# Attention by units of a head pair and 512 queries: the maxima are split on GpSimd, their rows copied by ScalarE, and the SyncE and GpSimd queues reordered

## The chip, the cores and the metric

The kernel is one program on one core of a Trainium2 chip. The metric is the device time of one execution in microseconds; lower is better. A core has five engines with a queue each: TensorE (PE, matmul), VectorE (DVE), ScalarE (ACT), GpSimd (POOL) and SyncE (SP, which here only issues DMAs). They meet through semaphores.

## The reference, cut to what matters

Four stages with a layer norm behind each: a linear recurrence, a mixture of eight experts, multi-head attention, and a gated feed-forward block with quantised operands. The batch is 4 sequences of 1024 tokens of width 256. Only the attention changes:

```python
zn = (z - mu) / jnp.sqrt(var + 1e-05) * ln_w + ln_b
qkv = (zn @ W_qkv + b_qkv).reshape(b, n, 3, H, DH)      # here b = 4, n = 1024, H = 16 heads, DH = 16
scores = jnp.einsum('bhqd,bhkd->bhqk', q, k) * scale     # scale = 1/4
attn = jax.nn.softmax(scores, axis=-1)
msa = jnp.einsum('bhqk,bhkd->bhqd', attn, v)
out = msa_cat @ W_proj + b_proj
```

## The kernel before, in words

The first two stages run once for all tokens (the first 450 us). Then each of the four sequences b runs attention and the feed-forward block, one after the other.

Heads go by pairs p = 0 to 7; head a of a pair uses its own half of TensorE's rows (partitions 64a and up). Queries and keys are kept as a high and a low part, stacked into 48 rows per head (tiles Qs and Ks, four buffers for the pairs). SyncE fills a buffer with 12 DMAs (`stack(p)`, L432; for pair 0 three of them are GpSimd's).

A softmax needs the maximum of each query's scores. The scores are computed twice. First with queries on the partitions, 128 queries by 512 keys at a time (`score_max`, L976): 32 such matmuls a pair, 256 a sequence, called maxima here. VectorE reduces each to one column of MX (L1546). When all 32 of a pair are reduced, VectorE takes the negated maximum (L1550), splits it into a rounded high and a low part (L1551, L1552), TensorE transposes the small tile NMs (`turn_max`, L983), VectorE copies the transposed rows to MR (L1559), and SyncE's two DMAs (`maxima_row`, L440) put them as rows 49 and 50 under the queries. Then the second computation has keys on the partitions and the maximum already subtracted (`transposed_scores`, L1006: 128 keys by 512 queries, one matmul for each head), ScalarE applies the exponential to both heads at once (L708), and TensorE weighs the values (`weigh`, L1019, 4 calls in the program and 8 matmuls in the trace). A pair has 8 key tiles and 2 query halves, so 16 steps of transposed scores, exponential, weigh; a sequence has 128 steps. This text numbers them n = 0 to 127. ScalarE copies a pair's sums out of bank 7 (`evac_o`, L681), and the next pair's first `weigh` waits for that.

The maxima run ahead of the steps. TensorE issues 38 of the 256 ahead of the first step: 32 of pair 0 between the eight `values` matmul groups (L960) and 6 of pair 1, with filling matmuls between them (`keep_warm`, L1028, whose results nobody reads; `fill`, L1033). Behind that it puts 5 maxima beside every two steps up to step 12, then 4, so two a step, until none is left; from step 24 on (FIRST = 12 key tiles) they alternate with the steps one by one ("apart"), before that by two steps together. Once the first steps have begun the maxima rotate through three PSUM banks (4, 5, 6). The transposition takes a place ("slot") in this rotation, and whoever issues slot i waits until the content of slot i - 3 has been read (`slot_free`). Before, VectorE reads all slots, so one counter `sld` serves.

GpSimd, when pair 7's stack has landed, fetches the next sequence's input (L482) and copies two small tiles (L484, L485), and at steps of its own choosing (counter `pv`) issues four groups of four gathers (L492), which VectorE needs behind the last maximum. SyncE's order is stack 0, 1, 2, row 0, stack 3, then row p - 3 and stack p in turn.

The lines on which the prediction leans, from the kernel before:

```python
    before = [k for k in range(max(0, i - 8), i) if slot_bank(k) == slot_bank(i)]   # slot_free
    return before[-1] + 1 if before else 0
...
    F["nms"].wait(pe, b, p + 1)                  # turn_max, TensorE
    F["sld"].wait(pe, b, slot_free(i))
```

## Time and profile before

| | us |
|---|---|
| median of 3 runs | 1757.94 (1756.63 to 1764.83) |
| the profiled execution, its own time | 1757.24 |
| its span, first to last instruction | 1755.2 |
| PE busy | 1589.3 (91%) |
| DVE busy | 1345.5 (77%) |
| ACT busy | 873.3 (50%) |
| POOL busy | 258.8 (15%) |

Busy time is a sum over instructions of an engine; matmuls are pipelined and overlap, so a busy TensorE is not one at its peak. The last column of some rows names what ended an engine's idle time. The granted TensorE clock is 0.962 of full speed as a mean over the span.

### The profile page before, as it was taken

The numbers are of one execution on the slowest core, as the hardware profiler recorded it, in microseconds if no ns is written. First come the engines' busy times: TensorE is split into PE (matmuls) and PEld (weight loads), VectorE is DVE, ScalarE is ACT, GpSimd is POOL, SyncE is SP. The second block draws the span as 40 slices with busy tenths as digits, with TensorE's granted clock in tenths as the row PEclk, the third lists the DMA queues.
The fourth block names the chain that finished last, engine by engine and source line by source line (L and its number), as shares of the span: only waits on it lengthen the run. The fifth ranks groups of instructions, "written<-read, shape, count | busy, mean of one in ns | idle before, by whom it ended". The sixth has DMA issues, their size and how long they took to land.

```text
span 1755.2 us, 28045 instructions
## 1 busy us (share of the span) xinstructions
PE 1589.3 (91%) x10730; PEld 965.1 (55%) x10730; DVE 1345.5 (77%) x2629; ACT 873.3 (50%) x1294; POOL 258.8 (15%) x255
## 2 busy tenths in 40 slices
PE   5987999995799998899999989999998999999795
PEld 1757899994353336565433557543336655333564
DVE  3575555542599986889998689899978989996696
ACT  1213444441347775153777723367782344778412
POOL 0144233223100120201003030100202010000020
PEclk8988999998799999999999989999998999999998
DMA  3126877784322310004222000322200032110000
GB/s 134 49 72 213 258 251 245 249 245 148 59 35 37 68 38 1 1 10 88 38 38 74 2 0 1 79 37 38 75 19 1 1 72 41 34 28 2 1 0 24
DMA packets 80175, 123.03 MB, mean 70 GB/s; under 512 B 13530, under 2 KB 55771, under 8 KB 80043
## 3 DMA queue, kind: packets, MB, share of 16 engines
q1 hardware_dynamic: 70666, 93.46, 20.4%
q0 software_dynamic: 9376, 27.80, 5.5%
q8 instruction: 85, 1.39, 0.3%
q14 instruction: 48, 0.39, 0.1%
HBM read 76.84 MB, written 18.61 MB: 54 GB/s over the span
## 4 chain that ended last, share of the span: by engine, by line
PE 76%; DVE 14%; ACT 4%; issue 3%; DMA 1%; POOL 1%; SPq 1%; DVEq 0%; ACTq 0%; POOLq 0%
PE PS L1019 14%; PE PS L976 13%; PE PS L901 7%; PE PS L1141 7%; PE PS L889 6%; PE PS L1006 6%; PE PS L1151 5%; DVE MX L1546 4%; PE PS L946 3%; PE PS L960 2%; ACT Pb L708 2%; PE PS L839 2%; PE PS L1028 2%; PE PS L1100 1%; PE PS L1177 1%
## 5 line engine op out<-in xcount | busy, mean ns | idle before, releaser
L1546 DVE TENSOR_REDUCE MX<-PS 128x1 f32<-128x512 f32 x1024 | 634.2, 682 | 37.1 <-PE PS L976 34.9
L708 ACT ACTIVATE Pb<-PS 128x1024 f32<-128x1024 f32 x512 | 509.0, 1025 | 171.2 <-PE PS L1006 167.7
L976 PE MATMUL PS<-Ks,Qs 48*128 48x512 f32 x1024 | 381.4, 456 | 13.6 <-DVE MX L1546 11.3
L1006 PE MATMUL PS<-Qs,Ks 50*128 50x512 f32 x1024 | 334.1, 455 | 14.2 <-ACT Pb L708 11.4
L1019 PE MATMUL PS<-Pb,V 128*32 128x256 f32 x4096 | 308.6, 390 | 1.2 <-ACT Pb L708 0.2
L976 PEld LDWEIGHTS PS<-Ks,Qs 48*128 48x128 f32 x1024 | 160.6, 184 | 220.0 <-DVE MX L1546 159.9
L1019 PEld LDWEIGHTS PS<-Pb,V 128*32 128x32 f32 x4096 | 90.4, 108 | 155.0 <-ACT Pb L708 75.4
L1006 PEld LDWEIGHTS PS<-Qs,Ks 50*128 50x128 f32 x1024 | 137.0, 185 | 50.2 <-ACT Pb L708 36.1
L901 PE MATMUL PS<-Pb,OT 128*128 128x256 f32 x624 | 141.0, 379 | 0.0
L889 PE MATMUL PS<-Ks,Qs 128*128 128x256 f32 x936 | 127.3, 294 | 6.3 <-DVE Ks L1426 6.3
L889 PEld LDWEIGHTS PS<-Ks,Qs 128*128 128x128 f32 x936 | 119.5, 197 | 8.6 <-DVE Ks L1426 7.5
L901 PEld LDWEIGHTS PS<-Pb,OT 128*128 128x128 f32 x624 | 115.8, 190 | 14.0
L1141 PE MATMUL PS<-wgT,XT 128*128 128x352 f32 x256 | 98.0, 535 | 15.3 <-DVE OT L1644 12.3
L473 POOL DMA_INDIRECT OT<-x_mid,idx x78 | 80.3, 1029 | 197.3 <-PE PS L878 158.9
L621 ACT ACTIVATE Qs<-Pb 128x1024 fp32r<-128x1024 f32 x39 | 41.3, 1060 | 120.4 <-DMA Pb<-W 120.4
L1151 PE MATMUL PS<-wdT,Pb 128*128 128x256 f32 (+1 forms) x384 | 96.1, 393 | 2.0 <-ACT Pb L761 2.0
L1151 PEld LDWEIGHTS PS<-wdT,Pb 128*128 128x128 f32 (+1 forms) x384 | 71.0, 192 | 26.6 <-issue 11.3
L632 ACT ACTIVATE OT<-PS,b1t 128x256 f32<-128x256 f32 x156 | 64.8, 470 | 38.6 <-PE PS L889 38.6
L1141 PE MATMUL PS<-wuT,XT 128*128 128x352 f32 x256 | 81.8, 463 | 0.0
L1141 PEld LDWEIGHTS PS<-wgT,XT 128*128 128x128 f32 x256 | 54.1, 222 | 44.3 <-DVE OT L1644 13.3
L738 ACT ACTIVATE OT<-PS 128x704 f32<-128x704 f32 x32 | 24.2, 756 | 104.5 <-PE PS L1141 104.5
L1422 DVE TENSOR_TENSOR Qs<-Pb,Qs 128x1024 fp32r<-128x1024 f32 x39 | 47.7, 1224 | 28.5 <-ACT Qs L621 28.0
(288 smaller groups left out, 1912.9 us busy)
## 6 DMA issues: line engine op xcount, KB each, us to landing
Pb<-W SPq DMA_DIRECT2D x78, 512.0 KB
y_slot<-V SPq DMA_DIRECT2D x39, 256.0 KB
Qs<-Qh SPq DMA_DIRECT2D x128, 64.0 KB, 2.3
Ks<-Kh SPq DMA_DIRECT2D x120, 64.0 KB, 2.3
V<-b SPq DMA_DIRECT2D x39, 128.0 KB
XT<-x_mid POOLq DMA_DIRECT2D x4, 1024.0 KB
out<-Pb POOLq DMA_DIRECT2D x4, 1024.0 KB, 6.7
OT<-xT SPq DMA_DIRECT2D x2, 1024.0 KB, 6.2
```

The costliest lines, as they stand in the source:

```text
L473: C[("xa", "xb", "xc")[k % 3]].inc(pool.indirect_dma_start(Xm[k % 3][:, a, :], None, x_mid[:, :], bass.IndirectOffsetOnAxis(idx[:, SA * k ...
L632: C["hr"].inc(act.activation(HTm[k % 2][:, hc, :], PS[:, 2 + 2 * (k % 2) + hc // 2, hc % 2 * ST:(hc % 2 + 1) * ST], ACT.Relu, bias=b1t[:, ...
L708: F["ex"].inc(act.activation(Pb[:, kt % 2, 2 * qh:2 * qh + 2, :], PS[:, 2 * qh:2 * qh + 2, :], ACT.Exp, scale=0.25))
L889: ins = pe.matmul(PS[:, 2 + 2 * (k % 2) + hc // 2, hc % 2 * ST:(hc % 2 + 1) * ST], w[k % 2][:, c, hc * P:(hc + 1) * P], x[k % 2][:, c, :], ...
L901: ins = pe.matmul(PS[:, 6 + k % 2, a * D:(a + 1) * D], HTm[k % 2][:, hc, a * P:(a + 1) * P], W2t[k % 2][:, hc, :], start=(hc == 0), stop=( ...
L946: ins = pe.matmul(o, wqkv[:, kc, w * D + c * P:w * D + (c + 1) * P], tokens, start=(kc == 0), stop=(kc == DC - 1))
L976: F["slp"].inc(pe.matmul(PS[:, slot_bank(i), :], Qs[rows, p % NB, t * P:(t + 1) * P], Ks[rows, p % NB, kh * HALF:(kh + 1) * HALF], start=T ...
L1006: ins = pe.matmul(PS[:, 2 * qh + a, :], Ks[rows, p % NB, kt * P:(kt + 1) * P], Qs[rows, p % NB, qh * HALF:(qh + 1) * HALF], start=True, st ...
L1019: ins = pe.matmul(PS[32 * j:32 * j + 32, 7, qh * QW:(qh + 1) * QW], V[:, kt, 2 * p + a, :], Pb[:, kt % 2, 2 * qh + a, c * QW:(c + 1) * QW] ...
L1141: ins = pe.matmul(PS[:, 2 * w + a, 0:IH], XT[:, c, t * P:(t + 1) * P], wT[:, c, a * IH:(a + 1) * IH], start=(c == 0), stop=(c == DC - 1))
L1151: ins = pe.matmul(PS[:, 6 + t % 2, 0:D], HT[0:k, c, :], wdT[0:k, c, :], start=(c == 0), stop=(c == IC - 1))
L1546: F["sld"].inc(dve.tensor_reduce(MX[:, p % 2, a, t, kh:kh + 1], PS[:, slot_bank(i), :], AX.X, ALU.max))
```

## The change

A unit is now a pair and 512 queries: 16 units u a sequence, of 16 maxima each (UN = 16). What was done once a pair is done once a unit:

- VectorE takes the negated maxima of the unit's four query tiles (one instruction, now issued one maximum late: behind maximum 16(u + 1), which is the next unit's first).
- GpSimd makes the high and the low part (`split_maxima`).
- TensorE transposes 16 rows instead of 32. The slot of unit u lies ahead of maximum 16(u + 1) + 6 (LATER = 6), for unit 0 ahead of maximum 17.
- ScalarE copies the rows to MR (`maxima_rows`), behind the exponential of the step in whose course the transposition is issued (`turn_step`), and raises a new counter `mrc`. The user of the slot three further on waits for `mrc` instead of `sld`.
- SyncE sends two DMAs a unit, on counters `mrow0` and `mrow1` by query half; steps 8u to 8u + 7 belong to unit u, so all 8 key tiles of one query half are now done before the other half.

The first step now comes behind 24 maxima (UN + START = 16 + 8). The values are no longer interleaved with filling matmuls; of `keep_warm` 2 + 7 * 3 are left. All steps are "apart", weigh of step n - 2 stands behind the transposed scores of step n, and at a pair's change weigh is left out of one step and done twice in the next. SyncE's order is stack 0, 1, row 0, stack 2, row 1, stack 3, row 2, then row, stack, row for each further pair. GpSimd's fetch and gathers now stand behind the splits of units 11 to 14.

```diff
-LEAD, START = 12, 6
-APART, PVS = 4, 2
-SOON, LATER = 1, 4
+LEAD, START = 14, 8
+GATHER = 11
+SOON, LATER = 1, 6
...
-        UN = 2 * TT * 2
-        SLOTS = NP * UN + NP
+        UN = 2 * TT
+        NU = 2 * NP
+        QT = TT // 2
+        SLOTS = NU * UN + NU
...
+        slot_use = {unit_slot(n): ("sld", n + 1) for n in range(NU * UN)}
+        slot_use.update({turn_slot(u): ("mrc", u + 1) for u in range(NU)})
...
-            return before[-1] + 1 if before else 0
+            return slot_use[before[-1]] if before else None
+
+        LAST = (NU * UN - UN - LEAD) // 2
+
+        def ahead_of(n):
+
+            return UN + min(LEAD + 2 * n, START + 5 * n // 2)
+
+        def turn_step(u):
+
+            if u + 1 == NU:
+                return LAST + 1
+            return next(n for n in range(NU * KT) if ahead_of(n + 1) > UN * (u + 1) + LATER)
...
-                for p in range(NB - 1):
+                stack(0)
+                stack(1)
+                maxima_row(0)
+                for p in range(2, NB):
                     stack(p)
-                maxima_row(0)
-                stack(NB - 1)
+                    maxima_row(p - 1)
                 for p in range(NB, NP):
-                    maxima_row(p - NB + 1)
+                    maxima_row(2 * (p - NB) + NB - 1)
                     stack(p)
-                for p in range(NP - NB + 1, NP):
-                    maxima_row(p)
+                    maxima_row(2 * (p - NB) + NB)
+                for u in range(2 * (NP - NB) + NB - 1, NU):
+                    maxima_row(u)
...
+                def split_maxima(u):
+
+                    F["neg"].wait(pool, b, u + 1)
+                    if u:
+                        F["slp"].wait(pool, b, turn_slot(u - 1) + 1)
+                    F["nmh"].inc(pool.tensor_copy(NMs[:, :, 0, :], NM[:, u % 2, :, :]))
+                    F["nmh"].wait(pool, b, u + 1)
+                    F["nms"].inc(pool.tensor_tensor(NMs[:, :, 1, :], NM[:, u % 2, :, :], NMs[:, :, 0, :].bitcast(F32), ALU.subtract))
+
+                for u in range(NU):
+                    split_maxima(u)
+                    if more and u == GATHER:
+                        F["vv"].wait(pool, b, TT)
+                        F[f"stk{NB - 1}"].wait(pool, b, NP // NB * STK)
+                        fetch(b + 1)
+                        F["cp"].wait(pool, b, 1, 1)
+                    if more and GATHER <= u < GATHER + TT // 2:
+                        gathers((u - GATHER,))
...
+                def maxima_rows(u):
+                    i = turn_slot(u)
+                    F["slp"].wait(act, b, i + 1)
+                    if u >= 2:
+                        F[f"mrow{u % 2}"].wait(act, b, 16 * 2 * (u // 2))
+                    F["mrc"].inc(act.activation(MR[:, u % 2, :], PS[0:2 * TT, slot_bank(i), 0:P], ACT.Copy))
+
+                maxima_rows(0)
+                for n in range(NU * KT):
+                    F["bp"].wait(act, b, n + 1)
+                    if n >= 4:
+                        F["pv"].wait(act, b, n - 3)
+                    F["ex"].inc(act.activation(weights_of(n), PS[:, 2 * (n % 2):2 * (n % 2) + 2, :], ACT.Exp, scale=0.25))
+                    if n > 2 and n % (2 * KT) == 1:
+                        evac_o(n // (2 * KT) - 1)
+                    for u in range(1, NU):
+                        if turn_step(u) == n:
+                            maxima_rows(u)
...
-                for t in range(1, TT):
-                    maxima(4 * t + 1)
-                    F["vv"].wait(pe, b, t)
-                    keep_warm(2, 1)
-                    maxima(4 * t + 3)
+                for t in range(1, 5):
+                    maxima(3 * t + 3)
                     values(t)
                 maxima(UN)
+                for t in (5, 6):
+                    values(t)
+                maxima(UN + SOON)
+                values(7)
                 F["vv"].wait(pe, b, TT)
-                keep_warm(18)
-                maxima(UN + SOON)
-                keep_warm(7, 1)
+                keep_warm(2, 1)
...
+                for n in range(NU * KT):
+                    if n == LAST + 2:
+                        turn_max(NU - 1)
+                    maxima(ahead_of(n) + 1)
+                    if n < 2:
+                        fill(2)
+                    transposed_scores(n)
+                    for k in range(ahead_of(n) + 2, ahead_of(n + 1) + 1):
+                        maxima(k)
+                        if n < 2:
+                            fill(2)
+                    if n < 2:
+                        continue
+                    if n == 2 or n % (2 * KT) != 2:
+                        if n > 3 and n % (2 * KT) == 3:
+                            weigh(n - 3)
+                        weigh(n - 2)
...
-                    link(dve.tensor_reduce(NM[:, :, :], MX[:, p % 2, :, :, :], AX.X, ALU.max, negate=True))
-                    link(dve.tensor_copy(NMs[:, :, 0, :], NM[:, :, :]))
-                    F["nms"].inc(dve.tensor_tensor(NMs[:, :, 1, :], NM[:, :, :], NMs[:, :, 0, :].bitcast(F32), ALU.subtract))
...
+                row_maxima(0, 1)
+                for u in range(NU):
+                    row_maxima(UN * u + 1, min(UN * (u + 1) + 1, NU * UN))
+                    negated_maxima(u)
```

## Rows read from the trace of the kernel before

**Rows 1.** The page's costliest group: busy us, mean ns, idle before

```profile
L1546 DVE TENSOR_REDUCE MX<-PS 128x1 f32<-128x512 f32 x1024 | 634.2, 682 | 37.1 <-PE PS L976 34.9
```

**Rows 2.** Second sequence by stretches: us, busy PE, PEld, DVE, ACT, POOL, clock, DMA

```profile
880.00:920.00 40.00, 39.90 (x364) 15.05 (x366) 38.67 (x69) 31.36 (x33) 0.00 (x0) 1.00 0.25 42
920.00:960.00 40.00, 38.56 (x339) 14.87 (x337) 35.99 (x65) 28.40 (x31) 13.74 (x17) 1.00 0.23 68
```

**Rows 3.** Timeline, one loop step (from 876.16), TensorE: start us, us, instruction

```profile
876.16 0.50 PE L976 MATMUL PS<-Ks,Qs 48*128 48x512 f32 x1
876.16 0.74 PE L1006 MATMUL PS<-Qs,Ks 50*128 50x512 f32 x2
...
876.83 0.64 PE L1019 MATMUL PS<-Pb,V 128*32 128x256 f32 x8
877.40 0.50 PE L976 MATMUL PS<-Ks,Qs 48*128 48x512 f32 x1
```

**Rows 4.** Timeline, the same step, ScalarE and VectorE

```profile
876.93 1.03 ACT L708 ACTIVATE Pb<-PS 128x1024 f32<-128x1024 f32 x1 [0.21 <-PE PS L1006]
...
875.46 6.25 DVE L1546 TENSOR_REDUCE MX<-PS 128x1 f32<-128x512 f32 x10
```

**Rows 5.** Timeline, start of attention, VectorE

```profile
796.54 19.22 DVE L1546 TENSOR_REDUCE MX<-PS 128x1 f32<-128x512 f32 x32
815.79 0.19 DVE L1550 TENSOR_REDUCE NM<-MX 128x16 f32<-128x32 f32 x1
...
817.14 0.28 DVE L1559 CAST MR<-PS 32x128 fp32r<-32x128 f32 x1
```

**Rows 6.** Timeline, the same stretch, TensorE

```profile
820.25 0.50 PE L1006 MATMUL PS<-Qs,Ks 50*128 50x512 f32 x2 [0.61 <-DMA Qs<-MR]
```

**Rows 7.** Timeline, the same stretch, SyncE's queue

```profile
808.11 0.59 SPq L432 DMA_DIRECT2D Ks<-OT  x1
817.45 1.36 SPq L440 DMA_DIRECT2D Qs<-MR  x2
```

**Rows 8.** Timeline, ScalarE, the last four exponentials of the sequence

```profile
989.45 3.78 ACT L708 ACTIVATE Pb<-PS 128x1024 f32<-128x1024 f32 x4 [0.19 <-PE PS L1006]
```

**Rows 9.** Groups by line and form, ScalarE and GpSimd: busy us, mean ns, idle

```profile
L761 ACT ACTIVATE Pb<-PS 64x128 f32<-64x128 f32 x32 | 8.6, 270 | 0.0
...
L485 POOL COPY svb<-sv 128x16 f32<-128x16 f32 x4 | 0.8, 204 | 0.0
```

**Rows 10.** Timeline, a transposition inside the loop, TensorE

```profile
903.54 0.50 PE L976 MATMUL PS<-Ks,Qs 48*128 48x512 f32 x1
...
905.17 0.28 PE L983 MATMUL PS<-ident,NMs 128*32 128x128 f32 x1
...
906.97 0.49 PE L976 MATMUL PS<-Ks,Qs 48*128 48x512 f32 x1
```

**Rows 11.** Timeline, TensorE, at steps 12, 24, 106 and behind the last

```profile
841.01 0.72 PE L1006 MATMUL PS<-Qs,Ks 50*128 50x512 f32 x2
...
857.20 0.40 PE L1006 MATMUL PS<-Qs,Ks 50*128 50x512 f32 x2
...
969.77 1.12 PE L1006 MATMUL PS<-Qs,Ks 50*128 50x512 f32 x4
...
991.87 2.05 PE L1019 MATMUL PS<-Pb,V 128*32 128x256 f32 x32
```

**Rows 12.** Timeline, TensorE, at a pair's change

```profile
891.93 0.49 PE L976 MATMUL PS<-Ks,Qs 48*128 48x512 f32 x1
...
894.86 0.50 PE L976 MATMUL PS<-Ks,Qs 48*128 48x512 f32 x1
```

**Rows 13.** Timeline, VectorE, last work before the heads' normalisation, and that

```profile
986.33 0.17 DVE L1483 TENSOR_SCALAR ve<-mv 128x8 f32<-128x8 f32 x1
995.77 0.26 DVE L1596 RECIPROCAL rc<-PS 128x16 f32<-128x16 f32 x1 [9.27 <-PE PS L1090]
```

**Rows 14.** The stack's line on SyncE's queue: min, median and max ns

```profile
L432 SPq DMA_DIRECT2D Qs<-Qh x128: 555/590/1837, 463.8 to 1554.2; - x128
```

More of the change, by code:

```diff
@@ L512, in sequence @@
             def sequence(b, more):
-                if more:
-                    F["vv"].wait(pool, b, TT)
-                    F[f"stk{NB - 1}"].wait(pool, b, NP // NB * STK)
-                    fetch(b + 1)
-                    F["cp"].wait(pool, b, 1, 1)
-                    for g in range(TT // 2):
-                        F["pv"].wait(pool, b, PVS * (APART * g + 5 * KT - 4))
-                        gathers((g,))
+                def split_maxima(u):
[14 more added lines that the diff above has]
+                        gathers((u - GATHER,))
                 w, nb = 2 * D, 2 * D // BLK
@@ L973, in score_max @@
                     if slot_free(i):
-                        F["sld"].wait(pe, b, slot_free(i))
+                        F[slot_free(i)[0]].wait(pe, b, slot_free(i)[1])
                     rows = slice(ROW * a, ROW * a + STACK)
@@ L988, in maxima @@
                 def maxima(upto):
-                    while issued[0] < min(upto, NP * UN):
+                    while issued[0] < min(upto, NU * UN):
                         n = issued[0]
@@ L997, in maxima, with transposed_scores @@
                         issued[0] += 1
-                def transposed_scores(p, kt, qh):
-                    n = 2 * (KT * p + kt) + qh
+                def transposed_scores(n):
+                    u, kt = n // KT, n % KT
+                    p, qh = u // 2, u % 2
+                    if kt == 0:
+                        F[f"mrow{qh}"].wait(pe, b, 16 * 2 * (p + 1))
                     if n >= 2:
@@ L1005, in transposed_scores, with weigh @@
                         rows = slice(ROW * a, ROW * a + MROWS)
-                        ins = pe.matmul(PS[:, 2 * qh + a, :], Ks[rows, p % NB, kt * P:(kt + 1) * P],
+                        ins = pe.matmul(PS[:, 2 * (n % 2) + a, :], Ks[rows, p % NB, kt * P:(kt + 1) * P],
                                         Qs[rows, p % NB, qh * HALF:(qh + 1) * HALF], start=True, stop=True)
                     F["bp"].inc(ins)
-                def weigh(m, qh):
-                    p, kt = m // KT, m % KT
-                    if kt == 0 and p:
+                def weigh(n):
+                    u, kt = n // KT, n % KT
+                    p, qh = u // 2, u % 2
+                    if kt == 0 and qh == 0 and p:
                         F["ov"].wait(pe, b, p)
-                    F["ex"].wait(pe, b, 2 * m + qh + 1)
+                    F["ex"].wait(pe, b, n + 1)
                     for c in range(2):
@@ L1053, in sequence @@
                 F["vm"].wait(pe, b, 1)
-                FIRST = 12
-                LAST = (NP * UN - UN - LEAD) // 4
-                for m in range(NP * KT):
-                    p, kt = m // KT, m % KT
-                    if kt == 0:
-                        F["mrow"].wait(pe, b, 16 * 2 * (p + 1))
-                    ahead = UN + min(LEAD + 4 * m, START + 5 * m)
-                    step = UN + min(LEAD + 4 * (m + 1), START + 5 * (m + 1)) - ahead
-                    apart = FIRST <= m < LAST
-                    for qh in range(2):
-                        if apart:
-                            maxima(ahead + 2 * qh + 1)
-                        transposed_scores(p, kt, qh)
-                        maxima(ahead + (2 if not qh else step if apart else 3))
-                        if m == 0:
-                            fill(2)
-                        if apart:
-                            weigh(m - 1, qh)
-                    if not apart:
-                        for qh in range(2 if m else 0):
-                            weigh(m - 1, qh)
-                        for n in range(ahead + 4, ahead + step + 1):
-                            maxima(n)
-                            if m == 0:
-                                fill(2)
-                        if m == LAST:
-                            turn_max(NP - 1)
-                for qh in range(2):
-                    weigh(NP * KT - 1, qh)
+                for n in range(NU * KT):
[8 more added lines that the diff above has]
+                        if n < 2:
+                            fill(2)
+                    if n < 2:
[4 more added lines that the diff above has]
+                        weigh(n - 2)
+                for n in range(NU * KT - 2, NU * KT):
+                    weigh(n)
                 F["ov"].wait(pe, b, NP)
```

85 lines of the change are left out of this document (33 added, 52 removed).

## The prediction

> **What bounds the kernel now.** I read the page first, then the chain of waits, then the busy time by stretches, and last the timeline of each engine in the second sequence (the four are alike; all times below are of it). The page's largest group is VectorE's reduction of the maxima [rows 1], but in the loop TensorE is busy for 39.90 of 40 us and VectorE for 38.67 [rows 2]: both are nearly full, TensorE a little more. The clock is granted in full in these stretches (1.00, the level of 2.4 GHz).
>
> One step of the loop shows why. It lasts 876.16 to 877.40, 1.24 us: a maximum and a transposed score start together, because they use different rows of the array, a second such couple follows, then weigh from 876.83 [rows 3]. VectorE takes 6.25 us for ten maxima, 0.62 each; unhindered it takes 19.22 / 32 = 0.60 [rows 4, 5]. ScalarE's exponential starts 0.77 us after the step's start and takes 1.03 [rows 3, 4], so it idles 0.21 a step.
>
> Ahead of the loop it is otherwise. VectorE begins at 796.54 and must do 32 maxima; the negation is at 815.79, the copy of the rows ends at 817.42, SyncE issues the row's DMAs at 817.45, and the first transposed score starts at 820.25, 2.83 us behind the copy [rows 5 to 7]. In these 24 us TensorE's filling matmuls do nothing useful. Behind the last maximum (step 106) the steps run by ScalarE: four exponentials in 3.96 us with the idle time ahead, 0.99 a step [rows 8].
>
> The sum is made against the profiled execution's own 1757.24 us (span 1755.2 and 2.0 around it), 0.7 under the median.
>
> **Part 1, the start and the catching up.** The first step needs 17 reductions instead of 33. 796.54 + 17 x 0.60 + 0.08 gives 806.8; the negation 0.19; GpSimd's two small instructions about 0.20 each, the nearest row being its copy of 128x16 [rows 9], with handovers 0.5 in all; TensorE's transposition 0.28 [rows 10]; ScalarE's copy about 0.27, by its copy of 64x128 out of PSUM [rows 9]. That is 808.3 with handovers. SyncE's queue holds only stacks 0 and 1 ahead of the row and has been past stack 2 at 808.7 even in the old order [rows 7], so it is free. With the same 2.83 us the first step could begin at 811.1; the 8 maxima ahead of it hold it to about 811.5. Before: 820.25, so 8.7 earlier.
>
> But 24 maxima have then been issued, not 38. Up to step 12 VectorE sets the pace: it starts again at about 808.4 with maximum 17, and 37 maxima bring it to 830.6; the second negation and the second transposition's slot add 0.5, and TensorE's lead takes as much off. Step 12 begins at 830.6 against 841.01 [rows 11]: **-10.4 us**.
>
> The negation runs off VectorE's path from here on: 0.2 a unit where it had 0.6 and a copy of 0.28 a pair.
>
> **Part 2, the transposition in the loop.** This is where I expect most of the gain to go. A transposition takes one of three slots. In the kernel before, VectorE frees it within its own order. The two steps from 903.54 to 906.97 with one of them inside take 3.43 instead of 2.48: 0.95 a pair [rows 10].
>
> Now ScalarE frees it, and its copy stands behind the exponential of the very step in which the transposition is issued. With the transposition's start as 0: the step's couples start at 0.21, its exponential at 0.21 + 0.77 = 0.98, the copy, overlapping the exponential's last 0.1 as the exponentials do (3.78 for four) [rows 8], runs 1.90 to 2.17. The third slot on is the first maximum of the next step, which TensorE would reach at 1.58 (1.24, the transposition's 0.21, and 0.13 by which VectorE's negation delays the second couple). It waits until 2.21 (a handover of 0.04, as between the copy at 817.42 and SyncE), and behind it in TensorE's queue wait the next transposed scores, and so the next exponential. Cost: 2.21 - 1.24 = 0.97 us a unit. The bounds: 0.34 if the wait isn't there, 1.3 if handovers are three times as long.
>
> A pair's change costs 2.93 - 2.48 = 0.45 now [rows 12]. Weigh left out of one step and doubled in the next lets ScalarE's copy of 0.6 pass; I take 0.2 (bounds 0 and 0.45).
>
> Steps 12 to 24: 12 x 1.24 + 2 x 0.97 + 0.2 = 17.0, before 857.20 - 841.01 = 16.2 [rows 11]: **+0.8**.
>
> Steps 24 to the last maximum: before 969.77 - 857.20 = 112.6 for 82 steps, which is 101.7 of steps, 5 x 0.95, 5 x 0.45 and 3.9 left over. The left-over lies where GpSimd issues gathers: TensorE's 39.90 of 40 us falls to 38.56 in that stretch [rows 2]; I keep it, since the gathers only move by nine steps. Now the last maximum is at step 113: 89 x 1.24 + 11 x 0.97 + 6 x 0.2 + 3.9 = 126.2. The tail before is 22 steps, from 969.77 to the end of the last weigh at 993.9 [rows 11], 24.1 = 22 x 0.99 + 2.3. Now 15 x 0.99 + 2.3 = 17.2. Together 143.4 against 136.7: **+6.7**.
>
> Sum: -10.4 + 0.8 + 6.7 = **-2.9 us a sequence, -11.6 in all: 1745.6**.
>
> **What I cost at nothing.** The next sequence's combination on VectorE ends at 986.33 and is wanted at 995.77 [rows 13]; it would start 4 us later (last maximum at 973.8 instead of 969.8), so end at 990.3, and be wanted 2.9 earlier, at 992.9: 2.6 us of cover are left; what is late beyond that counts in three of the four sequences. GpSimd: four gathers stand behind a unit's split, about 1 us each by its 13.74 us for 17 instructions [rows 2], and the next split is due 8 steps, 10 us, after. A unit's negation ends 1.45 into step 8u - 7 and the transposition stands at the start of step 8u - 4, 2.3 us on, of which the split takes 0.6: 1.7 to spare. Fetch now stands behind split 11, where pair 7's stack has landed. SyncE: a stack is 12 x 0.63 us by the row's median of 0.59 and a gap [rows 14], 9 with the row ahead of it; the next row is due 13 us after the last. The row in the loop: copy done 2.17 behind the transposition, 2.83 more for the DMA, 5.0; its reader is due at 2.21 + 3 x 1.24 = 5.93. Cover 0.9.
>
> GpSimd and VectorE might get into each other's way, which would undo the split's move. VectorE reads the maxima from PSUM while GpSimd works; in the stretch with gathers its mean for a maximum can't be told from that without [rows 2]. The Trainium skill (Perfetto Trace Analysis, "Optimizing Scalar/DVE Operations") warns that GpSimd and VectorE share an SBUF port, so that moving work between them might not help; SBUF — State Buffer, "Who interferes with whom", exempts a reduction on this chip. By the warning the move would gain VectorE nothing, by the exemption it costs nothing; the sum takes the second.
>
> **The rivals.** *A, the slot is free in time.* If the copy gets ahead of the exponential's end, or the slack absorbs it, a transposition costs 0.34: 13 x 0.63 and 0.3 at unit 1 are 8.5 a sequence, 34 in all: 1712. For it: ScalarE idles 0.21 a step. Against: that idle time lies ahead of the exponential, and the queue is in order. Chance 0.15.
>
> *B, slower: the rows come late.* Sixty times (15 a sequence) the steps wait for a row whose cover is 0.9 us. If a row takes 1.3 us longer inside the loop than at the start, 0.4 is lost each time, 24 us: 1770. It decides from 0.35 us a unit, where the sum reaches 1767. For it: single DMA issues took 1.84 instead of 0.59 [rows 14], and a row has two of them; fetch's 1 MB goes out close to row 11. Against: SyncE is otherwise idle then. Chance 0.12.
>
> *C, the two engines collide.* If VectorE stands still for GpSimd's 0.4 a unit, 16 x 4 x 0.4 = 26 us is the most; the wait behind the transposition, in which VectorE is idle for 0.63 anyway, should cover half: about 1758, no change. Chance 0.08.
>
> *D, the fillers are missed.* TensorE's clock stays at its higher level now while fillers run between the values. If it fell to the lower level for the first 12 steps, their matmuls would take twice as long, about 8 us a sequence: 1778. The gaps I see in the new order are under 0.5 us. Chance 0.03.
>
> **How the numbers follow.** My forecast has 0.62, with its own range 1735 to 1758 (0.1 us on each of 52 transpositions is 5 us; 1 us in a sequence's start is 4). Half a per cent, 8.8 us, is about what can be told from no change. Of the forecast 0.43 lies under 1749.2 and 0.19 within; with A faster is 0.58; with C and a part of B same is 0.28; slower 0.14, B and D. The range of 8 in 10 reaches to A below and to the edge of B above: 1709 to 1764. The predicted time is 1745.6.
>
> **What would show it.** Right: the first transposed score 15 us after VectorE's first maximum (23.7 now), give or take 1; behind each transposition the first maximum of the next step waiting 0.6 us for ScalarE; steps of 1.24; the last weigh 2.9 us earlier than now, counted from VectorE's first maximum. Wrong: no such wait (A); transposed scores waiting for the row's DMA at every eighth step (B); maxima of 0.7 us where GpSimd splits (C); steps longer than 1.24 without a wait.

## The result and the profile after

The changed kernel takes 1747.59 us in the median of its runs (1738.82 to 1770.11), the kernel before 1758.88 (1753.09 to 1764.83) beside it: a ratio of 0.9944, with a 95% interval of 0.9925 to 0.9963. Forecast were 1745.6 us, so -11.6 for a measured -11.3. The profiled execution took 1747.05 us, with a span of 1745.3: 9.9 less than before. A ratio here, and its interval, leave out the runs that lie over 1.5% above their kernel's fastest (here the one at 1770.11), and so can differ a little from the quotient of the medians.

The page's groups of VectorE's maxima, ScalarE's exponentials and TensorE's scores (busy us, mean ns, then the idle time ahead of them and who ended it) answer to [rows 1]; the last line is TensorE's own group in the page before:

```profile
L1581 DVE TENSOR_REDUCE MX<-PS 128x1 f32<-128x512 f32 x1024 | 636.5, 683 | 70.1 <-PE PS L1018 69.2
L748 ACT ACTIVATE Pb<-PS 128x1024 f32<-128x1024 f32 x512 | 518.9, 1026 | 180.0 <-PE PS L1051 179.4
L1018 PE MATMUL PS<-Ks,Qs 48*128 48x512 f32 x1024 | 389.8, 455 | 35.0 <-ACT MR L741 28.8
...
L976 PE MATMUL PS<-Ks,Qs 48*128 48x512 f32 x1024 | 381.4, 456 | 13.6 <-DVE MX L1546 11.3
```

A maximum costs what it did (683 ns against 682), but VectorE now idles 70.1 us ahead of them instead of 37.1. TensorE's maxima waited for VectorE before, 11.3 us in all. Now they wait for another engine: for 28.8 us TensorE stands still until ScalarE has copied a unit's rows.

The start of the second sequence, timeline of all engines (VectorE's first maximum is at 794.35; [rows 5 to 7] answer to it):

```profile
806.18 0.28 PE L1025 MATMUL PS<-ident,NMs 128*16 128x128 f32 x1
...
806.49 0.27 ACT L741 ACTIVATE MR<-PS 16x128 fp32r<-16x128 f32 x1 [0.80 <-PE PS L1025]
806.78 1.36 SPq L462 DMA_DIRECT2D Qs<-MR  x2
806.92 4.28 DVE L1581 TENSOR_REDUCE MX<-PS 128x1 f32<-128x512 f32 x7 [1.91 <-PE PS L1018]
...
810.15 0.50 PE L1051 MATMUL PS<-Qs,Ks 50*128 50x512 f32 x1
```

The first transposed score starts 15.80 us behind the first maximum, where it was 23.71: 7.9 earlier.

A step of the loop with a transposition in it, same view ([rows 10] answer to it):

```profile
873.11 0.28 PE L1025 MATMUL PS<-ident,NMs 128*16 128x128 f32 x1
...
874.09 1.02 ACT L748 ACTIVATE Pb<-PS 128x1024 f32<-128x1024 f32 x1 [0.42 <-PE PS L1051]
...
875.01 0.25 ACT L741 ACTIVATE MR<-PS 16x128 fp32r<-16x128 f32 x1
...
875.32 0.49 PE L1018 MATMUL PS<-Ks,Qs 48*128 48x512 f32 x1 [0.50 <-ACT MR L741]
```

From the transposition to the next step's first maximum it is 875.32 - 873.11 = 2.21 us. The copy stands behind the exponential in ScalarE's queue, and the maximum waits for the slot that the copy frees.

Counted from the first maximum to the start of ScalarE's last copy of the heads, the attention of the four sequences took 198.70, 197.45, 197.57 and 193.65 us before and takes 192.97, 193.46, 193.52 and 190.39: 17.0 less in sum. Some 1.2 of it is not the change's: in the kernel before the clock fell to 0.50 for 3.4 us (at 658.5) late in the first sequence. The span shows 9.9. The stretches between, which the change does not touch, came out 3.6 us longer ahead of the first sequence, 1.7 between them and 1.9 behind the last, in these two executions.

The last sequence is shorter in both kernels, and it alone issues no gathers for a next one. Timeline around the fourth gather of a unit, changed kernel, second sequence:

```profile
931.78 0.96 POOL L517 DMA_INDIRECT Kh<-y_slot,posb  x1 [0.30 <-issue]
...
933.56 2.48 DVE L1581 TENSOR_REDUCE MX<-PS 128x1 f32<-128x512 f32 x4 [1.29 <-PE PS L1018]
933.60 1.94 ACT L748 ACTIVATE Pb<-PS 128x1024 f32<-128x1024 f32 x2 [1.36 <-PE PS L1051]
934.30 0.50 PE L1018 MATMUL PS<-Ks,Qs 48*128 48x512 f32 x1 [0.65 <-DVE MX L1581]
```

VectorE and ScalarE, which read different banks, get nothing from TensorE for 1.29 and 1.36 us, and come back together 0.8 us after GpSimd's fourth gather has ended. The other three groups of gathers show the like: ScalarE comes back after 1.77, 1.09 and 1.75 us of idle time at 944.34, 955.75 and 967.63, each time 0.9 to 1.0 us behind a fourth gather's end, and VectorE beside it after 0.53, 1.50 and 0.51. I call this a stop below. Not all of this idle time is lost: at the three later places, behind a transposition, ScalarE is idle for 0.82 us in the fourth sequence too.

It is not bound to the fourth gather. In the third group ScalarE is late already before that one starts:

```profile
953.49 1.02 ACT L748 ACTIVATE Pb<-PS 128x1024 f32<-128x1024 f32 x1 [1.42 <-PE PS L1051]
953.83 0.96 POOL L517 DMA_INDIRECT Kh<-y_slot,posb  x1 [0.31 <-PE PS L1018]
```

This exponential comes 1.50 us behind the transposition (at 951.99). In the other two sequences with gathers the same one comes 1.54 and 1.53 behind it, in the fourth 0.97.

### The profile page after: what moved, and what is told of

Same layout as the page of the kernel before. It is cut to its first block, busy times and chain, and to the rows that moved or that the text cites. A ratio compares the mean times of both kernels' runs of the same rounds, so it can differ in the third digit from the quotient of the medians.

```text
span 1745.3 us, 28266 instructions
## 1 busy us (share of the span) xinstructions
PE 1568.2 (90%) x10646; PEld 940.9 (54%) x10646; DVE 1328.9 (76%) x2565; ACT 889.5 (51%) x1358; POOL 285.7 (16%) x383
## 4 chain that ended last, share of the span: by engine, by line
PE 71%; DVE 17%; issue 6%; ACT 3%; DMA 2%; POOL 1%; SPq 1%; ACTq 0%; DVEq 0%; POOLq 0%
PE PS L1065 13%; PE PS L1018 13%; PE PS L1176 7%; PE PS L943 7%; PE PS L931 6%; PE PS L1051 6%; DVE MX L1581 6%; PE PS L1186 5%; PE PS L988 3%; PE PS L1002 2%; PE PS L881 2%; PE PS L1135 1%; PE PS L1212 1%; DMA Pb<-W 1%; PE PS L920 1%
## 5 line engine op out<-in xcount | busy, mean ns | idle before, releaser
L1581 DVE TENSOR_REDUCE MX<-PS 128x1 f32<-128x512 f32 x1024 | 636.5, 683 | 70.1 <-PE PS L1018 69.2
L748 ACT ACTIVATE Pb<-PS 128x1024 f32<-128x1024 f32 x512 | 518.9, 1026 | 180.0 <-PE PS L1051 179.4
L1018 PE MATMUL PS<-Ks,Qs 48*128 48x512 f32 x1024 | 389.8, 455 | 35.0 <-ACT MR L741 28.8
L1051 PE MATMUL PS<-Qs,Ks 50*128 50x512 f32 x1024 | 360.4, 452 | 0.0
L1065 PE MATMUL PS<-Pb,V 128*32 128x256 f32 x4096 | 320.5, 390 | 0.5
L1065 PEld LDWEIGHTS PS<-Pb,V 128*32 128x32 f32 x4096 | 83.8, 108 | 162.0 <-ACT Pb L748 87.1
L1051 PEld LDWEIGHTS PS<-Qs,Ks 50*128 50x128 f32 x1024 | 143.5, 185 | 24.4 <-ACT Pb L748 19.8
L543 POOL CAST NMs<-NM 128x8 fp32r<-128x8 f32 x64 | 12.7, 199 | 597.7 <-DVE NM L1588 597.7
L1186 PEld LDWEIGHTS PS<-wdT,Pb 128*128 128x128 f32 (+1 forms) x384 | 71.0, 192 | 26.8 <-issue 11.3
```

The costliest lines, as they stand in the source:

```text
L748: F["ex"].inc(act.activation(weights_of(n), PS[:, 2 * (n % 2):2 * (n % 2) + 2, :], ACT.Exp, scale=0.25))
L1018: F["slp"].inc(pe.matmul(PS[:, slot_bank(i), :], Qs[rows, p % NB, t * P:(t + 1) * P], Ks[rows, p % NB, kh * HALF:(kh + 1) * HALF], start=T ...
L1051: ins = pe.matmul(PS[:, 2 * (n % 2) + a, :], Ks[rows, p % NB, kt * P:(kt + 1) * P], Qs[rows, p % NB, qh * HALF:(qh + 1) * HALF], start=Tru ...
L1065: ins = pe.matmul(PS[32 * j:32 * j + 32, 7, qh * QW:(qh + 1) * QW], V[:, kt, 2 * p + a, :], weights_of(n)[:, a, c * QW:(c + 1) * QW], star ...
L1186: ins = pe.matmul(PS[:, 6 + t % 2, 0:D], HT[0:k, c, :], wdT[0:k, c, :], start=(c == 0), stop=(c == IC - 1))
L1581: F["sld"].inc(dve.tensor_reduce(MX[:, p % 2, a, t, kh:kh + 1], PS[:, slot_bank(i), :], AX.X, ALU.max))
```

## The experiments

Twelve kernels ran, on three chips. The kernel before ran beside them at 1760.54 us in the first group of four, 1758.38 in the second and 1748.87 in the third; each ratio is to its own. A unit's time is the distance between two splits of the maxima, read in the profiled execution (so a split that GpSimd issues late shifts it); "units 11 to 14" are those with gathers behind them.

### First group: which part of the change costs what

**The changed kernel again.**

> The changed kernel itself, as the yardstick of this call. Ratio to the kernel before 0.994 (0.992 to 0.996), as in its own timing.

1749.24 us (1740.08 to 1753.63), ratio 0.9924 [0.9900, 0.9949]. A unit without gathers alternates between 11.13 and 10.87 us, 22.00 for two. In this execution something is new. Windows in the third sequence (us, busy PE, PEld, VectorE, ScalarE, GpSimd, granted clock, DMA share, GB/s):

```profile
1260.00:1270.00 10.00, 8.73 (x81) 3.43 (x76) 7.94 (x14) 7.23 (x9) 4.22 (x6) 0.97 0.18 53
1270.00:1280.00 10.00, 10.00 (x60) 3.30 (x52) 6.03 (x12) 4.34 (x5) 2.73 (x5) 0.50 0.05 15
```

Behind a group of gathers the granted clock falls to 0.50, the level of 1.2 GHz, for 30.7 us (1269.3 to 1300.0). That sequence took 204.7 us of attention instead of 193.5.

**The copy ahead of the exponential** (units 2 to 14; the lines `+` come before the wait for the step's scores):

```diff
 for n in range(NU * KT):
+    for u in range(2, NU - 1):
+        if turn_step(u) == n:
+            maxima_rows(u)
     F["bp"].wait(act, b, n + 1)
...
     F["ex"].inc(act.activation(weights_of(n), ...))
...
-    for u in range(1, NU):
+    for u in (1, NU - 1):
         if turn_step(u) == n:
             maxima_rows(u)
```

> The changed kernel with ScalarE's copy of the rows of units 2 to 14 ahead of the exponential of the same step instead of behind it. ScalarE is idle for 0.21 us there and the transposition is done 0.7 us before that exponential can start, so by my theory the wait of TensorE for the slot goes and a transposition costs about 0.34 us instead of 0.97: 13 x 0.63 = 8 us a sequence, 33 in all, so about 0.975 of the kernel before. The rival (the slot's wait only takes the place of time that VectorE needs for its maxima anyway) expects no change: 0.994. In between, if VectorE becomes the limit at 16 x 0.62 a unit.

1747.2 us (1731.4 to 1775.56), ratio 0.9893 [0.9865, 0.9922], where 0.975 was expected. Timeline, a step with a transposition:

```profile
874.28 0.28 PE L1028 MATMUL PS<-ident,NMs 128*16 128x128 f32 x1
...
874.73 0.25 ACT L741 ACTIVATE MR<-PS 16x128 fp32r<-16x128 f32 x1
...
875.26 1.02 ACT L751 ACTIVATE Pb<-PS 128x1024 f32<-128x1024 f32 x1 [0.28 <-PE PS L1054]
...
875.91 0.49 PE L1021 MATMUL PS<-Ks,Qs 48*128 48x512 f32 x1
```

From the transposition to the next maximum it is 1.63 us instead of 2.21, with no wait. Two units take 20.65 instead of 22.00, and the undisturbed fourth sequence 181.94 instead of 190.47: 8.5 us less, which is what the prediction's rival A asked for (8.5 a sequence). The time shows little of it, because the first three sequences gave it back (198.49, 196.03 and 206.39 us). Windows of the second:

```profile
920.00:930.00 10.00, 10.00 (x93) 3.95 (x93) 9.11 (x16) 7.96 (x10) 4.99 (x9) 1.00 0.37 119
930.00:940.00 10.00, 8.90 (x56) 2.77 (x48) 6.35 (x11) 4.77 (x5) 2.62 (x5) 0.63 0.15 47
940.00:950.00 10.00, 10.00 (x57) 3.39 (x53) 5.33 (x10) 4.60 (x6) 2.23 (x3) 0.50 0.17 50
950.00:960.00 10.00, 10.00 (x61) 3.75 (x59) 6.32 (x11) 5.60 (x6) 3.80 (x6) 0.51 0.10 30
```

and the timeline at its beginning:

```profile
931.44 1.89 DVE L1584 TENSOR_REDUCE MX<-PS 128x1 f32<-128x512 f32 x3 [1.47 <-PE PS L1021]
931.49 1.94 ACT L751 ACTIVATE Pb<-PS 128x1024 f32<-128x1024 f32 x2 [1.81 <-PE PS L1054]
932.19 0.18 PEld L1021 LDWEIGHTS PS<-Ks,Qs 48*128 48x128 f32 x1 [1.54 <-DVE MX L1584]
932.19 0.51 PE L1021 MATMUL PS<-Ks,Qs 48*128 48x512 f32 x1 [1.10 <-DVE MX L1584]
```

A stop, 1.10 us of idle TensorE behind it, and then the lower clock from 932.5 to 959.9, in which TensorE is busy for 10.00 of 10 us and does 57 to 61 matmuls where it had done 93.

**The rows' copy on VectorE, as before the change.** `maxima_rows` moves from ScalarE's loop to VectorE's, just ahead of the maximum whose slot follows the transposition.

> The changed kernel with the copy of the rows given back to VectorE, in its order just ahead of the maximum whose slot follows the transposition, as in the kernel before; the split stays on GpSimd. By my theory the place of the copy behind the exponential is what costs, so this gains too: VectorE does 16 x 0.60 + 0.2 + 0.25 = 10.05 us a unit, TensorE 9.92 + 0.34 = 10.26, a transposition costs 0.4 to 0.6: 5 to 7 us a sequence, 0.980 of the kernel before. If ScalarE's copy was right to relieve VectorE (rival), this is slower than the changed kernel: over 0.994.

1746.95 us, from only four runs: 1728.51 and 1732.74 at a mean clock of 0.946, 1761.15 and 1764.85 at 0.928 and 0.920. Too few and too far apart for a ratio; 0.980 was expected, and the two quicker runs are at 0.983. The fourth sequence took 181.76 us, the others 189.24, 195.91 and 195.97 with the same falls of the clock behind gathers. Who copies does not matter, then; that the copy is not behind an exponential does.

**The split on VectorE, as before the change.**

```diff
-F["nmh"].inc(pool.tensor_copy(NMs[:, :, 0, :], ...))
-F["nms"].inc(pool.tensor_tensor(NMs[:, :, 1, :], ...))
+F["nmh"].inc(dve.tensor_copy(NMs[:, :, 0, :], ...))
+F["nms"].inc(dve.tensor_tensor(NMs[:, :, 1, :], ...))
```

> The changed kernel with the split of the maxima given back to VectorE, the copy of the rows stays on ScalarE. It puts 0.4 us a unit on VectorE. By my theory VectorE is idle behind each transposition for 0.6 us anyway, so that inside the loop it costs little, 0 to 0.15 us a unit, and the first transposition comes a little earlier: within 0.992 to 1.000 of the kernel before. If the move of the split is what the change lives on (rival), each unit costs 0.4 more: 25 us, 1.008.

1773.42 us (1771.82 to 1777.55), ratio 1.0083 [1.0065, 1.0101]: slower than the kernel before. Two units take 22.66 us, 0.33 more each; the two instructions are 0.17 each. I had counted them as covered by VectorE's idle 0.6 us behind a transposition, and expected 0.992 to 1.000; none of them is covered. The split stands two steps ahead of the transposition (at 872.82, the transposition at 875.45), and the idle time comes only behind it; that the maxima held up there are what costs is my reading, no run isolated it. That is some 4 us a sequence (197.3 against 193.5). The rest of the 24 us to the changed kernel goes with the clock: all four runs have a mean granted clock of 0.950 to 0.952, where runs of the changed kernel reach 0.963 to 0.965, and in the profiled one it fell for 34 us behind unit 1's transposition in the fourth sequence, far from any gather. Ahead of that fall TensorE had waited only 0.18 and 0.24 us for VectorE.

### Second group: the gathers

Three kernels with the copy ahead, and one of another question.

**One row a gather, plain.** In the attention each of the 16 gathers becomes `pool.dma_start(dst[0:1, t, :], y_slot[r:r + 1, :])`.

> The row copy stands ahead of the same step's exponential, as in the copy-ahead kernel (where a unit without gathers took 10.33 us instead of 11.00), and each of the 16 gathers of the next sequence's rows that GpSimd issues within the attention brings one row by a plain transfer instead of 128 by index (the next sequence computes on rows that are not its own; the work is the same). Theory (the gathers stop both readers of PSUM for 1 to 2 us, and TensorE's granted clock falls to its lower level behind such a stop): units 11 to 14 take 10.33 us too, no stretch of the attention at the lower clock, the attention 182 us in all four sequences, the median 1712 to 1718 us and the runs within 8 us of each other. Rival (TensorE, with no gap left between its matmuls, is throttled for being busy, whatever the transfers do): the lower clock still shows in the loop, times of 1730 to 1775 us as widely spread as with the full gathers (1731 to 1776).

1705.95 us (1703.79 to 1707.16), ratio 0.9683 [0.9660, 0.9706]. (The next sequence then computes on rows that are not its own.) Attention 182.39, 182.59, 182.11 and 182.03 us; units 12 to 14 at 10.31, 10.37 and 9.80, and the clock at 1.00 in all four attentions. The theory holds and the rival (TensorE throttled for being busy) falls, since TensorE has no more gaps than in the copy-ahead kernel. That kernel ran on the chip of the first group and this one on another; that this chip makes stops and falls too is seen in the changed kernel's form with weighing in every step, below. The time came out 6 to 12 us under what I had written: 1745.6 - 34 for the waits left the stops of three sequences, 3.1 us each, in the sum.

**All rows, plain.** As above with `dst[:, t, :]` and 128 rows.

> As the kernel above, but each of the 16 gathers is a plain transfer of the same 128 rows of 1 KB, issued by GpSimd too (the next sequence computes on rows that are not its own). If the bytes on the DMA engines cause the stop: units 11 to 14 stay at 10.9 to 12.4 us, and the clock falls in the first three sequences, median 1735 to 1755. If the index form causes it (what GpSimd does for one, or packets of 1 KB from scattered rows): as with one row, 1712 to 1722 us. I expect the first with 6 in 10.

1701.21 us (1698.68 to 1705.93), ratio 0.9654 [0.9626, 0.9681]. I had expected the stops to stay, at 6 in 10; they are gone (units 12 to 14: 10.30, 10.32, 9.80), though the bytes are the same, and the queue shows 128 packets of 4096 bytes a group for both forms. So it is not the amount of traffic. What differs is how GpSimd makes the transfer and that the indexed rows lie scattered; the run does not part the two. Timeline of GpSimd:

```profile
941.74 0.55 POOL L518 DMA_DIRECT2D Qh<-y_slot  x1
942.28 0.55 POOL L518 DMA_DIRECT2D Kh<-y_slot  x1
942.83 0.54 POOL L518 DMA_DIRECT2D Qh<-y_slot  x1
943.36 0.54 POOL L518 DMA_DIRECT2D Kh<-y_slot  x1
```

Here four stand closer behind each other (0.54 us) than four by index (1.27), and ScalarE's idle time ahead of the exponentials at 941.94 and 943.17 is the loop's own 0.20. Unit 11, with the fetch of 1 MB, still has 11.20 to 11.44 us. There the prediction's rival B is at work: the transposed score at 918.10 waits 0.60 us for its row's DMA.

**The index gathers, two steps apart**, with the copy ahead.

```diff
 for t in (2 * g, 2 * g + 1):
     for k, dst in enumerate((Y1, Y2)):
+        if step is not None and (t % 2 or k):
+            F["bp"].wait(pool, at_b[0], step + 2 * (2 * (t % 2) + k))
         F[f"gat{g}"].inc(pool.indirect_dma_start(dst[:, t, :], ...))
...
-gathers((u - GATHER,))
+gathers((u - GATHER,), turn_step(u))
```

> The copy-ahead kernel with its four gathers of a unit two steps of the loop apart (GpSimd waits for the count of transposed scores between them) instead of one behind the other. It computes all. Theory (what stops the readers is the queue of packets of several gathers behind each other: the stop came behind the fourth): the stops shrink from 1.4 to 1.8 us to under 0.5, units 11 to 14 take 10.3 to 10.9 us, falls of the clock become rare, median 1714 to 1728 us. Rival (each gather by itself makes a stop): units 11 to 14 stay at 11 to 12 us or more, clock falls stay, median 1735 to 1760.

1703.12 us (1696.75 to 1706.0), ratio 0.9665 [0.9637, 0.9693]: 3.35% under the kernel before, the lowest ratio of the kernels that leave nothing out, and 11 us below the range that I had written (1714 to 1728). Attention 182.93, 182.98, 184.40 and 181.91 us. Timeline of GpSimd, and the same windows as above:

```profile
932.36 0.95 POOL L521 DMA_INDIRECT Kh<-y_slot,posb  x1 [2.83 <-PE PS L1060]
934.84 0.95 POOL L521 DMA_INDIRECT Qh<-y_slot,posb  x1 [1.52 <-PE PS L1060]
937.32 0.95 POOL L521 DMA_INDIRECT Kh<-y_slot,posb  x1 [1.53 <-PE PS L1027]
```

```profile
920.00:930.00 10.00, 10.00 (x97) 3.88 (x94) 9.78 (x17) 8.48 (x10) 4.25 (x6) 1.00 0.18 54
930.00:940.00 10.00, 10.00 (x97) 3.70 (x96) 9.58 (x18) 7.95 (x10) 4.25 (x6) 1.00 0.20 55
```

TensorE is busy for 10.00 of 10 us at the full clock with the gathers running beside it, units 12 and 13 at 10.30 and 10.37. The last maximum ends 166.0 to 166.1 us behind the first in all four sequences, with gathers or without, so the gathers cost the loop nothing. A gather by index does no harm by itself; several behind each other do. Two are not enough: a unit's fourth gather and the next unit's first start 1.6 us apart (926.94 and 928.53), and there is no stop behind them.

The spacing has a price of its own, though. The last unit's split stands on GpSimd behind the spaced fourth gather, and the last transposition waits for it:

```profile
947.38 1.18 POOL L521 DMA_INDIRECT Kh<-y_slot,posb  x1 [1.29 <-PE PS L1060]
...
949.20 0.28 PE L1034 MATMUL PS<-ident,NMs 128*16 128x128 f32 x1 [1.10 <-POOL NMs L551]
```

That wait of 1.1 us is in all three sequences with gathers and not in the fourth (0.08), and accounts for their 1.0 us more. In the third the clock also fell for 3.4 us right behind it: 184.40.

**Weighing in every step.** `weigh(n - 2)` in each step of the changed kernel, none left out at a pair's change and doubled behind it.

> The changed kernel, but TensorE weighs the values of step n-2 in every step: it does not leave a pair's first weighing for the step behind, where it does two. The prediction took a pair's change at 0.2 us above the two transpositions (a pair of units 22.0 us: 16 steps of 1.24, twice 0.97 and 0.22). Theory: the first weighing of a pair then waits for ScalarE's copy of the pair before (0.59 us, issued behind an exponential), so a pair takes 22.2 to 22.8 us, 7 such changes in each of 4 sequences, the time 6 to 20 us above the changed kernel's. Rival (the copy is there in time, and the doubled weighing itself costs the 0.22): a pair takes 21.8 us, the time 0 to 6 us below.

1746.88 us (1743.14 to 1765.22), ratio 0.9942 [0.9914, 0.9971], not to be told from the changed kernel's 0.9944; 6 to 20 us above it were expected. In the profile two units take 22.17 instead of 22.00, and the fourth sequence 191.99 instead of 190.47: the leaving out is worth 0.15 to 0.2 us a pair, which is below what the median can show. This kernel ran on the chip of the three above and has the stops (units 11 to 14 of the third sequence: 11.98, 11.40, 12.14, 10.88, where the spaced kernel has 10.92, 10.30, 10.30, 10.29), and a fall of the clock for 51 us in the first sequence (215.08 us).

### Third group: what the spacing does alone

**Spacing in the changed kernel, nothing else.**

> The changed kernel with its four gathers of a unit two steps of the loop apart, and nothing else (ScalarE's copy of the rows still behind the same step's exponential). Theory: units 11 to 14 fall from 12.4, 11.4, 12.0, 10.9 us to 11.6 (the fetch of the rows costs some 0.6), 10.9, 11.1, 10.9, which is 2 to 2.5 us a sequence; no clock falls in the attention; the median 1736 to 1741 us, and the runs within 10 us of each other instead of 30. Rival (the copy-ahead order and the spacing only work together): 1742 to 1750 us as spread as before.

1734.7 us (1731.63 to 1737.18), ratio 0.9915 [0.9895, 0.9934]. Units 11 to 14 at 11.73, 10.87, 11.13 and 10.86, as the theory had them; the attention 193.01, 191.40, 191.40 and 190.42 us, so some 2 us a sequence less than the changed kernel's 193.5. The 193.01 has a fall of the clock of 3.4 us in it (at 650.6), behind the same wait of 1.10 us for the last split. The mean clock of every run lies between 0.960 and 0.964, and the six runs 5.6 us apart (the changed kernel's six in the first group 13.6, its twenty 31).

The ratio itself proves little: its interval overlaps that of the changed kernel repeated (0.9900 to 0.9949), and the changed kernel did not run on this chip.

**Spacing in the kernel before, nothing else** (a wait for two more weighings ahead of each gather of a group but the first).

> The kernel before the change with its four gathers of a group two weighings apart, and nothing else. Its sequences with gathers took 197.5 to 198.7 us of attention, the one without 193.65. Theory (the same stops): 2.5 to 3.5 us less in each of three, the median 1748 to 1753 us. Rival (the stops of the kernel before lay under other waits): within 3 us of 1758.

1747.57 us (1744.7 to 1752.61), ratio 0.9992 [0.9977, 1.0007]. By the ratio the rival holds, by the profile the theory: the attention takes 193.86, 193.71, 193.75 and 193.74 us, so the stops (11.4 us in sum in the profiled execution of before) are gone. What fits both is that the kernel before had no stops on this chip: it ran there at 1748.87, 9.5 to 11.7 us less than on the other two. There is no profile of it from this chip, so this is a reading and not shown.

**Gathers in twos**, copy ahead, four steps between the twos.

> The copy-ahead kernel with the four gathers of a unit in two groups of two (GpSimd waits four steps between the groups, none within one). If the stop needs a queue of more than two gathers: 1703 to 1708 us, units as in the kernel with all four apart. If the second gather behind the first is enough: a stop of 0.5 to 1.5 us in each group, units 12 to 14 at 10.6 to 11.5 us, median 1710 to 1735 us. I expect the first with 5 in 10.

1700.61 us (1695.59 to 1703.47), ratio 0.9717 [0.9690, 0.9743], units 12 to 14 at 10.31, 10.39 and 9.79: no stop. If this chip made none in the kernel before either, it says nothing of how many gathers a stop needs. What does is the second group's spaced kernel (two, 1.6 us apart, make none) and the changed kernel's third groups (late before the fourth begins). The last transposition does not wait for its split here (0.08 us), since the fourth gather follows the third at once.

**The split on VectorE**, copy ahead, gathers apart.

> The kernel with the copy ahead and the gathers apart, but the split of the maxima on VectorE again (two instructions of 0.17 us a unit, from GpSimd). A unit takes 10.33 us there, in which VectorE is busy for 96 of 100. Theory (VectorE has little room in the unit, and the negated maxima of a unit stand in the chain of the PSUM slots): 0.2 to 0.4 us of the 0.40 show in each unit, 10.5 to 10.7 us, the median 13 to 26 us above 1703. Rival (VectorE catches up within the unit): 10.33 us, within 4 us of 1703.

1732.22 us (1729.29 to 1735.8), ratio 0.9897 [0.9873, 0.9921]: 29 us above the spaced kernel, where 13 to 26 were expected (on another chip, so by the times only roughly). Timeline of VectorE:

```profile
1119.27 0.16 DVE L1594 TENSOR_REDUCE NM<-MX 128x8 f32<-128x16 f32 x1
...
1119.46 0.17 DVE L1598 CAST NMs<-NM 128x8 fp32r<-128x8 f32 x1
...
1119.67 0.17 DVE L1600 TENSOR_TENSOR NMs<-NM,NMs 128x8 fp32r<-128x8 f32 x1
1119.75 3.87 DVE L1587 TENSOR_REDUCE MX<-PS 128x1 f32<-128x512 f32 x6
```

Two units take 21.50 instead of 20.65, 0.42 each: the whole price of 0.40 that was expected at most. And the clock falls although no gather is near; windows from the third sequence's catching up:

```profile
1112.00:1122.00 10.00, 9.79 (x69) 5.44 (x65) 9.93 (x20) 5.87 (x6) 0.00 (x0) 1.00 0.49 80
1122.00:1132.00 10.00, 9.76 (x52) 3.65 (x51) 6.40 (x11) 3.49 (x5) 0.00 (x0) 0.53 0.44 73
```

It falls at 1122.5, behind unit 1's transposition at 1121.78, and stays down for 34 us. Ahead of it TensorE waits 0.19 us for VectorE, and behind it 0.24. The spaced kernel has the same 0.19 there and no fall, so the short waits alone do not explain it. That sequence took 199.92 us, the others 187.69 to 187.75.

## Why the prediction was right, step by step

**The sum.** Per sequence, second sequence of both profiles, counted from VectorE's first maximum:

- The start. Forecast: the first transposed score 8.7 us earlier. It is 7.9. Step 12 begins at 829.32, 34.97 behind the first maximum instead of 44.47: -9.5 for a forecast -10.4. Most of the missing 0.9 is one wait: VectorE starts its next run of maxima at 806.92, 12.57 us behind the first maximum and after 1.91 us of waiting, where the sum had it back after 808.4 - 796.54 = 11.9.
- Steps 12 to 24. 846.16 - 829.32 = 16.84 against 16.19: +0.65 for +0.8.
- From there to the last maximum (971.23): 125.1 us for a forecast 126.2 (its terms add to 126.1); the tail to the end of the last weigh (987.75) 16.5 for 17.2. Together 141.6 for 143.4: +4.9 instead of +6.7. Of the 1.8 that are missing, 0.8 is the gathers' left-over, below.
- Sum -4.0 where -2.9 was forecast. The four sequences gave -5.7, -4.0, -4.1 and -3.3, the first of them with the 1.2 us of clock in the kernel before. No run put the old start back: its 9.5 us are read from the two timelines.

**The transposition** is the step that carries the forecast, and it is as written down: 2.21 us from it to the next maximum, the releaser is ScalarE's copy, and 16 steps take 846.93 to 868.93 = 22.00, which is 19.84 + 2 x 0.97 + 0.22, the 0.22 being what is left for the pair's change. Waits of the changed kernel in the loop, 846.93 to 912.9 (us in total, times, longest):

```profile
PEld PS L1018 <- ACT MR L741: 6.5, 6, 1.2
...
PE PS L1018 <- ACT MR L741: 3.6, 6, 0.7
```

Six units, six such waits, 0.6 us of idle TensorE each. The copy-ahead kernel removed it and the fourth sequence became 8.5 us shorter: mechanism and price are shown. So rival A failed as a forecast of this kernel, and was right about what its condition is worth.

**The pair's change** was put at 0.2; 0.22 is left for it in the profile, and weighing evenly costs 0.15 to 0.2 more.

**The costs at nothing.** No transposed score of the profiled execution waits for a row's DMA, so rival B's cover of 0.9 us held; the rests between sequences are 123.8 us (123.8, 123.8 and 122.1 before), so the combination was in time. The 112 maxima that run beside a split of GpSimd's take 680 ns, the others 684, so C does not show here. The Trainium skill (Perfetto Trace Analysis, "Optimizing Scalar/DVE Operations") warns that work moved between GpSimd and VectorE might not help. Here it did: the split on VectorE cost 0.33 to 0.42 us a unit, and on GpSimd none of it showed inside the loop.

**The gathers** were the weak place. I carried their left-over of 3.9 us over as a number, without asking what it is. Its size roughly held (193.5 - 190.4 = 3.1). What I did not see is that a stop can drop the clock: by the runs' clocks, the 31 us between the changed kernel's fastest and slowest run are mostly that. Its runs with a mean granted clock of 0.961 to 0.965 lie at 1738.8 to 1747.1 us, the slowest has 0.940 and 1770.1. In its profiled execution no fall lies inside the attention, in the repeated one a single fall cost 11.2 us. Rival D had a fall of the clock, but in the first 12 steps of a sequence, where neither profiled execution of this kernel has one. The forecast of -11.6 contains no falls and met a median that contains some; the repeat of 1740.08 to 1753.63 shows how far such a median can move. That the total came within 2 us is therefore partly luck: the sum over the sequences was 5.4 us too small a gain, and the untouched stretches and the clock took about as much back.

**The kernel before** hardly shows such falls: its runs in the first group all have clocks of 0.959 to 0.964 and lie within 8.0 us, in the second all but one (1768.19 at 0.956) within 7.1, though it has such stops too. Why the changed kernel is more exposed was not isolated. The nearest hint is how long TensorE itself stands still beside the gathers: at most 0.75 us in the profile of the kernel before, 1.19 to 1.25 in each such sequence of the changed kernel's two, and 1.07 to 1.17 ahead of each fall of the two kernels in which the copy is not behind an exponential. But most of the changed kernel's waits of that length had no fall behind them, and the falls in the kernel with weighing in every step and in the two with the split on VectorE came behind waits of 0.5 us or less.

**What stays open:** by what the stop comes about (the readers of PSUM lose TensorE's results for a while, after index gathers behind each other, and not after plain ones, whether for the index form or for the scattered rows); whether three gathers are enough, as the late exponential at 953.49 suggests; whether it depends on the chip; and what makes the clock fall behind one wait and not behind another.

## What to carry to other kernels

When a buffer's release moves to another engine, work out where in that engine's queue the release stands, not how long it takes: 0.25 us of copy behind an exponential cost 0.6 to 0.7 us a unit, and ahead of it none of that. A left-over in a stretch with GpSimd's index gathers is worth an experiment of its own; spread over the steps they cost the loop nothing here, only 1 us a sequence for the last split that then stood behind one of them, and with the copy moved as well the kernel gained 3.35% instead of 0.6%. Read the granted clock of each run beside its time before you explain a spread or a median.

## What the hardware showed that I had not expected

- Behind four index gathers issued 1.27 us apart (0.96 each), ScalarE gets nothing from TensorE for 1.1 to 1.8 us (up to 0.8 of it the loop's own) and VectorE for 0.5 to 1.5; four plain transfers of the same bytes 0.54 apart do not do this, nor do index gathers 2.5 us apart, nor two of them 1.6 us apart.
- Behind such a stop, with 1.10 us of idle TensorE, the granted clock went from 1.00 to 0.50 and stayed there for 27 us, although TensorE was busy for 10.00 of 10 us in between. Over the kernels with such gathers it stayed down for 7 to 51 us.
- The clock also fell behind unit 1's transposition when VectorE had the split (34 us in both kernels, no gathers near), in a stretch in which TensorE was busy for 9.79 of 10 us, with waits of 0.19 and 0.24.
